# Graph attention layers: block transposes on VectorE and 32 SBUF to SBUF DMAs per item in place of TensorE transposes

## The reference

```python
si = x @ attn_w[l, :d]; sj = x @ attn_w[l, d:]
scores = si[:, :, None] + sj[:, None, :] + attn_b[l]
scores = where(scores >= 0, scores, 0.2 * scores)      # then -inf off the mask
attn = softmax(scores); agg = attn @ x
h = layernorm(x + agg, g1[l], beta1[l])
x = layernorm(h + gelu(h @ W1[l] + b1[l]) @ W2[l] + b2[l], g2[l], beta2[l])
```

## Time and profile before

| | |
|---|---|
| median of 3 runs | 1281.48 us (1281.45 to 1281.96) |
| profiled execution | 1281.6 us |
| its span, first to last instruction | 1279.8 us |
| granted PE clock | 0.997 of full speed |
| DMA packets, mean rate | 52944 packets, 41 GB/s |

### The profile page before, as it was taken

The page is one execution under the profiler, slowest core; times in us unless marked ns, Lnnn a source line. Parts: engine busy times, 40 slices in busy tenths (PEclk is TensorE's granted clock), DMA queues, the critical chain, the costliest instruction groups (busy, mean ns, idle before and its releaser), DMA issues.

```text
span 1279.8 us, 23042 instructions
## 1 busy us (share of the span) xinstructions
PE 1240.6 (97%) x7877; PEld 1122.5 (88%) x7877; DVE 1110.3 (87%) x3331; ACT 917.7 (72%) x1754; POOL 652.5 (51%) x535
## 2 busy tenths in 40 slices
PE   3899999999999999999999999999999999999997
PEld 1799999988899999999889999999989899989996
DVE  7888888899998788889998888789999888888765
ACT  4777777677876776678777776777778766776663
POOL 1435553556555534554566445544666355435563
PEclk9999999999999999999999999999999999999998
DMA  7111111112220001011230000002321100000111
GB/s 248 53 33 43 26 26 34 34 51 66 67 67 10 10 10 17 10 34 51 75 100 26 9 18 10 9 10 43 99 75 42 34 10 9 10 17 26 26 41 58
DMA packets 52944, 52.31 MB, mean 41 GB/s; under 512 B 9272, under 2 KB 45148, under 8 KB 52828
## 3 DMA queue, kind: packets, MB, share of 16 engines
q1 hardware_dynamic: 52828, 50.85, 14.4%
HBM read 42.36 MB, written 8.48 MB: 40 GB/s over the span
## 4 chain that ended last, share of the span: by engine, by line
PE 77%; DVE 18%; ACT 2%; issue 2%; DMA 1%; POOL 0%; DVEq 0%; POOLq 0%
PE acc L955 35%; PE hbank L940 33%; PE acc L969 5%; DVE hid_lo L541 3%; PE util L990 3%; DVE xs L680 2%; PE util L1000 1%; DVE xs L667 1%; DVE st L528 1%; DVE st L674 1%; DVE ve L519 1%; DVE mv L517 1%; DVE st L562 1%; DVE junk L627 1%; DVE sc L654 1%
## 5 line engine op out<-in xcount | busy, mean ns | idle before, releaser
L955 PE MATMUL acc<-w2hi,hid_hi 128*128 128x256 f32 x1536 | 446.0, 290 | 0.0
L813 ACT ACTIVATE hbank<-hbank,vec 128x512 f32<-128x512 f32 x384 | 253.7, 661 | 266.5 <-PE hbank L940 262.0
L955 PE MATMUL acc<-w2hi,hid_lo 128*128 128x256 f32 x1536 | 434.9, 283 | 0.0
L955 PE MATMUL acc<-w2lo,hid_hi 128*128 128x256 f32 x1536 | 434.4, 283 | 0.0
L389 POOL TENSOR_TENSOR rstd<-ve,halfs 128x4 f32<-128x4 f32 x111 | 120.1, 1082 | 492.1 <-DVE ve L519 487.2
L940 PE MATMUL hbank<-ht_hi,w1hi 128*128 128x512 f32 x768 | 311.2, 405 | 2.8 <-DVE hid_lo L541 1.4
L955 PEld LDWEIGHTS acc<-w2hi,hid_hi 128*128 128x128 f32 x1536 | 293.8, 191 | 10.5
L940 PE MATMUL hbank<-ht_lo,w1hi 128*128 128x512 f32 x768 | 302.6, 394 | 0.0
L955 PEld LDWEIGHTS acc<-w2lo,hid_hi 128*128 128x128 f32 x1536 | 293.7, 191 | 8.8
L940 PE MATMUL hbank<-ht_hi,w1lo 128*128 128x512 f32 x768 | 300.8, 392 | 0.0
L955 PEld LDWEIGHTS acc<-w2hi,hid_lo 128*128 128x128 f32 x1536 | 293.5, 191 | 0.0
(11 more groups left out here) (76 smaller groups left out, 1740.3 us busy)
## 6 DMA issues: line engine op xcount, KB each, us to landing
sj_bc<-sj_dram SPq DMA_DIRECT2D x47, 256.0 KB, 3.9
xraw<-in_x_dram SPq DMA_DIRECT2D x16, 512.0 KB, 4.4
out_dram<-xout SPq DMA_DIRECT2D x32, 256.0 KB, 4.4
xres<-in_x_dram SPq DMA_DIRECT2D x15, 512.0 KB, 5.6
xout<-in_L_gnn_W_dram SPq DMA_DIRECT2D x10, 512.0 KB, 5.0
adji<-in_adj_dram SPq DMA_DIRECT2D x16, 256.0 KB, 2.9
ln_rows<-in_L_gnn_g_dram SPq DMA_DIRECT2D x2, 384.0 KB, 8.0
ln_rows<-in_L_gnn_beta_dram SPq DMA_DIRECT2D x2, 384.0 KB, 7.6
```

What stands on the lines that cost most here:

```text
L813: act.activation(hbank[k % HB][:], hbank[k % HB][:], ACT.Gelu, bias=b1c(i.l, c)).then_inc(gelu_n, 1)
L955: mm = pe.matmul(to, v[:, k % HID, of_g], w[:, i.l, c], start=c == 0 and n == 0 and g % HG == 0, stop=c == C - 1 and n == 2, skip_group_ch ...
```

## The change

- Items 0 and 1 keep the transposes on PE (`BY_PE = 2`). From item 2 on, `turn_e` and `turn_z` on DVE turn each 32x32 block of E (128x512) and of the normed rows (128x1024) in place of its block position, and `move_e` and `move_z` on SP bring the blocks to their partitions: 16 DMAs for E, each of 32 partitions with one run of 512 B, and 16 for the rows, each of 32 partitions with two runs of 512 B. `et_out` on ACT goes for these items, and `h_out` reads SBUF in place of PSUM.
- `norm1` moves from DVE to ACT, as x times rstd plus a shift that one small DVE instruction (`shift1`) makes. `add_bias` goes into the start value of `i_dots`. The row maximum comes out of `masked` (now four instructions that also reduce) and two instructions on 128x4 take the place of `minus_max`. Four small instructions of `input_shift` become one. The sum of variance and epsilon moves from DVE to POOL.
- Aggregation has two PSUM banks of its own (`mix`), and ffn2 has two in place of four.
- The order is written anew on every engine. An item's E is now turned, moved and aggregated in the slot in which it is a, and the rows in the slot in which it is b; the slot of PE begins with `ffn1(f, 3)`.

The core of the diff (of each slot the new order alone, its removed lines left out; the engine is put behind the name):

```diff
 PENS = 4
 EARLY = 1
 LEAD = 3
+BY_PE = 2
+QD = 32
+NQ = P // QD
+MOVES = 16 * NQ * NQ
+MOVES_Z = MOVES
 Item = namedtuple("Item", "q l g")
...
-        ET = sb("ET", [P, GG, P])
+        ET = sb("ET", [P, NQ, QD, GG])
+        te = sb("te", [P, NQ, QD, GG])
+        tz = sb("tz", [P, KD * NQ, GG, QD])
+        zt = sb("zt", [P, KD, NQ, GG, QD])
...
-        acc = [psum(f"acc{i}", [P, HG, D]) for i in range(4)]
+        acc = [psum(f"acc{i}", [P, HG, D]) for i in range(HG)]
+        mix = [psum(f"mix{i}", [P, HG, D]) for i in range(HG)]
         util = psum("util", [P, TOK])
-        def acc_of(i, h): return acc[2 * (i.q % 2) + h]
+        def acc_of(i, h): return acc[h]
+        def mix_of(i, h): return mix[h]
...
+        def moved(q):
+            return q - BY_PE + 1
...
+            def move_e(i):
+                if i.q < BY_PE:
+                    return
+                sp.wait_ge(te_n, moved(i.q))
+                sp.wait_ge(agg_n, 2 * i.q)
+                for a in range(NQ):
+                    for b in range(NQ):
+                        sp.dma_start(ET[b * QD:(b + 1) * QD, a], te[a * QD:(a + 1) * QD, b]).then_inc(et_in, 16)
+            def move_z(i):
+                if i.q < BY_PE:
+                    return
+                sp.wait_ge(tz_n, moved(i.q))
+                sp.wait_ge(ht_n, KD * i.q)
+                by_half = tz[:].rearrange("p (m b) g t -> p m b g t", m=KD)
+                for a in range(NQ):
+                    for b in range(NQ):
+                        sp.dma_start(zt[b * QD:(b + 1) * QD, :, a], by_half[a * QD:(a + 1) * QD, :, b]).then_inc(zt_in, 16)
...
             def slot(s):  # sync
+                o, t, b, a, d, p, n = item(s - 2), item(s - 1), item(s + 1), item(s + 2), item(s + 3), item(s + 4), item(s + 5)
+                if b:
+                    move_z(b)
+                if a:
+                    move_e(a)
+                if t and t.l == L - 1:
+                    load_xres(t)
                 if d:
                     send_sj(d)
                     load_sj(d)
+                load_weights(s + 6)
+                if p and p.l == 0:
+                    load_adj(p)
+                if o and o.l == L - 1:
+                    send_out(o, 1)
+                if t and t.l == L - 1:
+                    send_out(t, 0)
+                if n and n.l == 0:
+                    load_xraw(n)
+                if s == ITEMS - 4:
+                    load_last_input()
...
-                pool.wait_ge(ve_n[n], q + 1)
+                pool.wait_ge(mv_n[n], GG * (q + 1))
                 if n == "0":
                     wait(pool, x0_n, GG * q)
+                pool.tensor_scalar(ve[n][:], mv[n][:, :, 1], EPS, None, ALU.add).then_inc(ve_n[n], 1)
+                pool.wait_ge(ve_n[n], q + 1)
...
             def slot(s):  # gpsimd
+                t, f, b, a, p = item(s - 1), item(s), item(s + 1), item(s + 2), item(s + 4)
+                if b:
+                    h_gamma(b, 0)
+                if f:
+                    h_beta(f, 0)
+                    h_beta(f, 1)
+                if b:
+                    h_gamma(b, 1)
                 if t:
                     make_rstd("2", t.q)
+                if p and p.l == 0:
+                    make_rstd("0", p.g)
                 if t:
                     x_gamma(t, 0)
                     x_beta(t, 0)
                     x_gamma(t, 1)
+                    x_beta(t, 1)
+                if t and t.l == L - 1:
+                    add_input(t, 0)
+                    add_input(t, 1)
+                if a:
+                    make_rstd("1", a.q)
...
+                wait(dve, leaky_n, GG * (i.q - 1))
+                wait(dve, below_n, i.q - 1)
+                for g in range(GG):
+                    last = dve.tensor_tensor_reduce(junk[:, g], x_of(i)[:, g], attn_rows[:, i.l, 0], 1.0,
+                                                    attn_bias[:, i.l:i.l + 1], ALU.mult, ALU.add,
+                                                    si_of(i)[:, g:g + 1])
...
             def masked(i):
                 dve.wait_ge(pen_n, i.g + 1)
-                wait(dve, et_n, i.q)
+                wait_e_turned(dve, i.q - 1)
                 if i.q == 0:
                     dve.wait_ge(sj_n, 1)
                     row = util[:].rearrange("p (g j) -> p g j", g=GG)
                 else:
                     dve.wait_ge(sj_in, 16 * i.q)
                     row = sj_bc[:].rearrange("p j g -> p g j")
-                dve.tensor_tensor(sc[:], pen[:, i.g % PENS], row, ALU.min).then_inc(mask_n, 1)
+                for g in range(GG):
+                    last = dve.tensor_tensor_reduce(sc[:, g], pen[:, i.g % PENS, g], row[:, g], 1.0, -BIG, ALU.add,
+                                                    ALU.max, msj[:, g:g + 1])
+                last.then_inc(mask_n, 1)
             def minus_max(i):
-                dve.wait_ge(leaky_n, GG * (i.q + 1))
-                dve.tensor_reduce(negm[:], sc[:], AX_X, ALU.max, negate=True).then_inc(negm_n, 1)
+                dve.wait_ge(mask_n, i.q + 1)
+                dve.wait_ge(dots_n, i.q + 1)
+                wait(dve, exp_n, GG * i.q)
+                dve.scalar_tensor_tensor(out=below[:], in0=msj[:], scalar=-1.0, in1=si_of(i), op0=ALU.mult,
+                                         op1=ALU.subtract).then_inc(below_n, 1)
+                dve.wait_ge(below_n, i.q + 1)
+                dve.scalar_tensor_tensor(out=negm[:], in0=below[:], scalar=SLOPE, in1=below[:], op0=ALU.mult,
+                                         op1=ALU.min).then_inc(negm_n, 1)
+            def turn_e(i):
+                if i.q < BY_PE:
+                    return
+                dve.wait_ge(exp_n, GG * (i.q + 1))
+                wait(dve, et_in, MOVES * (moved(i.q) - 1))
+                dve.transpose(te[:].rearrange("p b i g -> p b g i"), sc[:].rearrange("p g (b j) -> p b g j", j=QD)).then_inc(te_n, 1)
+            def turn_z(i):
+                if i.q < BY_PE:
+                    return
+                dve.wait_ge(z1_n, GG * (i.q + 1))
+                wait(dve, zt_in, MOVES_Z * (moved(i.q) - 1))
+                dve.transpose(tz[:], x_of(i).rearrange("p g (c j) -> p c g j", j=QD)).then_inc(tz_n, 1)
...
-                    dve.scalar_tensor_tensor(out=x_of(i)[:, g], in0=acc_of(i, h)[:, g % HG],
+                    dve.scalar_tensor_tensor(out=x_of(i)[:, g], in0=mix_of(i, h)[:, g % HG],
...
-            def norm1(i):
+            def shift1(i):
                 dve.wait_ge(rstd_n["1"], i.q + 1)
-                for g in range(GG):
-                    dve.tensor_scalar(x_of(i)[:, g], x_of(i)[:, g], mv["1"][:, g, 0:1], rstd["1"][:, g:g + 1],
-                                      ALU.subtract, ALU.mult).then_inc(z1_n, 1)
+                wait(dve, z1_n, GG * i.q)
+                dve.scalar_tensor_tensor(out=nmr1[:], in0=mv["1"][:, :, 0], scalar=-1.0, in1=rstd["1"][:],
+                                         op0=ALU.mult, op1=ALU.mult).then_inc(nmr1_n, 1)
...
             def slot(s):  # vector
                 if t:
+                    residual(t, 0)
                     residual(t, 1)
+                if b:
+                    turn_z(b)
+                if f:
+                    low(f, 2)
                 if a:
+                    minus_max(a)
                 if t:
                     moments2(t)
                 if f:
+                    low(f, 3)
+                if p and p.l == 0:
+                    input_moments(p)
+                if a:
+                    turn_e(a)
+                split_weights(s + 4)
                 if t:
                     norm2(t, 0)
                 if d and d.l == 0:
                     penalty(d)
+                if f:
+                    low(f, 4)
                 if t:
                     norm2(t, 1)
                 if b:
                     h_low(b, 0)
                 if f:
                     low(f, 5)
+                if p and p.l == 0:
+                    input_shift(p)
+                if f:
                     low(f, 6)
                 if b:
                     h_low(b, 1)
                 if d:
                     j_dots(d)
+                if a:
+                    attend(a, 0)
+                    attend(a, 1)
                 if f:
+                    low(f, 7)
+                if a:
+                    moments1(a)
+                if b:
+                    low(b, 0)
+                if d:
+                    i_dots(d)
+                if a:
+                    shift1(a)
+                if d:
+                    masked(d)
+                if b:
+                    low(b, 1)
...
-                               scale=g1c(i.l, m)).then_inc(ht_n, 1)
+                if i.q < BY_PE:
+                    act.wait_ge(zt_n, KD * i.q + m + 1)
+                    if i.q == 0 and m == 0:
+                        act.wait_ge(vec_ready, 1)
+                    act.activation(util[:], util[:], ACT.Identity, bias=beta1c(i.l, m),
```

(133 more changed lines are left out.)

301 lines of the change are left out of this document (100 added, 201 removed).

## The result

The changed kernel takes 1752.72 us (median of 4 runs, 1747.5 to 1757.07) against 1281.72 us (4 runs, 1281.45 to 1282.57): a ratio of 1.3672, with a 95% interval of 1.3632 to 1.3711. The forecast was 1302 us with a range of 1232 to 1345. The direction was right, the size wrong by a factor of more than twenty, and the time lies far outside the range. The profiled execution took 1751.2 us, its span is 1749.4 us, and the granted clock 0.852 of full speed, where it had been 0.997.

A forecast was written before the change was run, and what follows sets the result against it. A loop through SP's DMA issues bounds each slot: 10.85 + 0.1 + 12.45 + 1.4 + 0.1 + 0.87 = 25.8 us against 25.71. With +4 over 44 slots and +17 for output slots, 1302 us, range 1232 to 1345.

The forecast's parts named there:

- The direction: Whole kernel: forecast slower than before, 1302 us, with a chance of 0.56 for slower.
- the price of an issue: SP's DMA issues: 0.43 us each for move_z, 0.37 for move_e, 12.45 us until E's last DMA begins to issue.
- the forecast's 25.8: One slot's loop through DVE, SP and PE, summed to 25.8 us.
- Rival 2: SP's loop much longer because closely following issues wait: 0.444 each, a slot of 27.1, 1360 us; chance 0.20.
- stand for 1.5 us: PE before aggregate(a, 0): idle 1.5 us in each slot, waiting for ET.
- the loop through SP: Every slot: DVE's work, SP's issues, E's landing and PE's first half of aggregation run one after another, 25.8 us.
- PE's work without the transposes: PE's slot: three groups of transposes, 1.32 us of 25.61, go, leaving 24.3 us.
- DVE's tail: DVE from the aggregation's first half to the end of turn_z: 10.85 us, plus 0.1 for the handover to SP.
- Landing and wake: After E's last DMA begins to issue: 1.4 us until it lands and 0.1 until PE wakes up.
- The 1.1 us for slots that write a group: The 15 slots that write a group: the loop grows by about 1.1 us there, 17 us in all.
- rival 1: PE stays the bound because 32-partition DMAs issue cheaper, 0.31 us each: loop 22.9, 1220 us; chance 0.37.

The follow-up runs named there:

- probe: The kernel before with up to sixteen extra DMAs a slot on SP, of twelve forms, on tiles that nothing reads: 1321.2 us, a single execution.
- dram_hop: The changed kernel with E and the rows each exchanged through DRAM, one store and four loads in place of 16 direct DMAs: 1255.33 us, ratio 0.9792.
- hop_z: The changed kernel with only the rows through DRAM (one store, four loads), E's 16 direct DMAs left as they are: 1537.77 us, ratio 1.1995.
- e_pe: The changed kernel with E's transposes back on PE and the order fitted, the rows still by sixteen DMAs: 1506.7 us, ratio 1.1755.
- e_on_act: The changed kernel with E's 16 DMAs issued by ACT in place of SP, which keeps the rows' 16: 1745.64 us, a single execution.
- hop_e: The changed kernel with only E through DRAM (one store, four loads), the rows' 16 direct DMAs left as they are: 1475.33 us, ratio 1.1508.

## Why the prediction was wrong

**The step that failed is the price of an issue.** "move_e has the first form, 0.37 each; move_z, with two runs per partition, the second, 0.43 each", bounded by 0.31 and 0.44. It measured 0.64 from start to start for both, outside the bounds, and 31 of them are 19.88 us in place of 12.45: 7.4 of the 9.5 us by which this slot exceeds the forecast's 25.8. The bounds were drawn from DMAs with one side in DRAM, and the form of the pattern was taken as what sets the price. Between move_e and move_z it makes no difference (medians of 591 and 597 ns); at the same pattern, the places of the two ends do (0.59 against 0.42 in the probe). The pattern can matter all the same, as the 0.61 and 0.43 of dram_hop's loads show. Rival 2 had part of the mechanism, issues that follow each other closely cost more, with 0.444; the probe shows that step (0.51 to 0.59), but also the larger one that no row of before could show. Its 0.444 was misread as well: the 5.77 us from 0.74 to 6.51 hold thirteen issues and so twelve distances, 0.48 each. That would have made rival 2 a slot of 28.2, still 7 short of the measured one. The text should have said that a DMA between two SBUF tiles is an operation without a row, and have widened the bounds accordingly.

**The second term that was missing is PE's clock.** The forecast let PE stand for 1.5 us and then work as before. It stood for 5.27 and then ran at 0.50: the first half took 2.21 for 0.87, and DVE waited 0.75 for the second. That is 1.34 + 0.75 = 2.1 us a slot in the loop, less about 0.2 for the reading of ET with a step (the whole aggregation takes 1.96 at full clock in dram_hop's chain, for 1.73). No run has such a pause without the slow clock behind it, so the division is worked out from rows, not shown by itself.

**What held.** The mechanism: the loop through SP sets the slot, PE waits before the first aggregation matmul with a DMA on ET as the last to come, and DVE waits before attend. PE's work without the transposes: 24.3 was forecast, and slots of 24.15 to 24.5 appear wherever the loop is short. turn_z 1.24 (1.2), four `masked` 1.25 (1.3), DVE's tail 11.34 with the 0.75 in it (10.95). Landing and wake 1.86 (1.5), too short by 0.4. turn_e took 1.11 for 0.8, beside the path.

**What was wrong without weight.** The 1.1 us for slots that write a group can't be seen in the changed kernel: its slots around 730 to 940 us lie between 35.2 and 37.1 whether they read, write or neither. Where PE bounds, such slots cost 2 us more than quiet ones (26.28 against 24.16 in dram_hop). That is the larger part of why dram_hop gains 27 us and not the 62 that rival 1 has for a PE bound everywhere: over the last 44 distances of the sj stores, from 63.2 to 1172.1, its slots exceed 24.3 us by 40 us in all, 24 of them where a group is read or written. The other 16 lie in slots of up to 26.2 that do neither, and their cause is open.

**The two readings of the Trainium skill.** The Trainium skill says that the sequencer's time is usually small beside the DMA ("DMA: Bandwidth & Descriptors", section "Issuing engines are not separate DMA queues"). This stood beside rival 1 and doesn't hold here: 0.59 us of issue stand beside a landing of 1.8, and sixteen issues follow one another while landings overlap. The Trainium skill's 512 cycles of earlier generations (same page, section "Why a DMA increments its semaphore by 16 and not by 1") are 0.43 us as an estimate, at the 1.2 GHz of "Advanced Engine Details and Errata", section "Clock Domains". That lies near the 0.42 of the probe's DRAM forms in a row and well below the 0.59 of the direct ones.

## What to carry to other kernels

Count the DMAs on the path before their bytes: thirty-two issues of 0.64 us are twenty microseconds of one engine, and a detour through DRAM with ten DMAs was 9.8 us where the direct way with thirty-two was 20.5. Before a price is taken from a row, ask whether the ends lie in the same kinds of memory, whether the row stood alone or in a burst, and whether the pattern has as many dimensions; if no row agrees, the operation has no row. Before an order is fitted, follow the loop once round: hop_z and e_pe missed because a piece of DVE's list in the loop had not been counted. And where a new wait stops PE for several microseconds, add the slower matmuls behind it to the sum.

## What the runs showed of the hardware that was not expected

- A DMA issue on SP between two SBUF tiles (probe): 0.51 us with each waiting for the last to land, 0.59 plus 0.04 to the next in a row, within 0.58 to 0.60 for 1 to 128 partitions and 16 to 512 B in each. With one side in DRAM: 0.42 in a row, 0.30 to 0.32 at the fastest; but 0.61 for a load of eight runs per partition, where one of four runs took 0.43 (dram_hop).
- The sj store to DRAM right behind such a burst took 0.53 to issue (the changed kernel), alone 0.32 (the kernel before).
- SP and ACT issue side by side at 0.63 and 0.65 us each (e_on_act).
- After pauses of PE of 5.27 us (the changed kernel), 4.66 us (hop_z) and 2.93 us (hop_e) the granted clock of the next 2.9 to 4 us was 0.50 (1.2 GHz), in the changed kernel then 0.99 (2.4 GHz).
- Block transposes on DVE in float32: 1.24 us for 128x1024, 1.11 us for 128x512 written with a step of 16 B (means of 46 each in the changed kernel).
